# Routed experts in tiles of two widths, and expert offsets added to the ranks by a matmul

## The reference, cut to what matters

```python
gate = xf @ gate_w                                   # 4096 x 8
weights, sel = jax.lax.top_k(gate, k=2)
weights = jax.nn.softmax(weights, axis=-1)
h = einsum('ecd,td->tec', dense_1_w, xf) + dense_1_b  # 256 -> 2*512, each expert
h = swiglu(h)
y = einsum('edf,tef->ted', dense_2_w, h) + dense_2_b  # 512 -> 256
out = sum over the two selected experts of weight * y
x = x + gb * out
```

## Time and profile before

| | |
|---|---|
| median of 3 runs | 625.39 us (624.7 to 627.05) |
| profiled execution, its own time | 623.77 us |
| its span, first to last instruction | 622.0 us |
| TensorE busy | 566.1 us, 91% |
| VectorE busy | 492.8 us, 79% |
| POOL busy | 318.5 us, 51% |
| chain that ended last | 67% PE, 22% DVE |

### The profile page before, as it was taken

How to read it: one execution, slowest core, us unless ns; L and a number is a source line. 1 busy time by engine, 2 the same in 40 slices (tenths; PEclk the granted TensorE clock), 3 DMA queues, 4 the chain that set the end, 5 groups by cost and what they waited for, 6 DMA issues and landing times.

```text
span 622.0 us, 13215 instructions
## 1 busy us (share of the span) xinstructions
PE 566.1 (91%) x4005; PEld 429.5 (69%) x4006; DVE 492.8 (79%) x1067; ACT 300.9 (48%) x497; POOL 318.5 (51%) x211
## 2 busy tenths in 40 slices
PE   5998999999999967459899999999999999999982
PEld 5444555655656534326788888888888888888871
DVE  1258879899999899897588888888888888888881
ACT  3677568789688762732433333333333333333320
POOL 0004031442414421002458888888888888888554
PEclk9799889899899886776899999999999999999996
DMA  9204273653645448533667777777777777777633
GB/s 316 95 18 170 68 202 102 202 144 115 199 102 170 119 129 308 175 29 95 157 101 138 137 137 137 138 134 132 128 137 134 135 133 134 135 131 130 95 35 35
DMA packets 86942, 82.93 MB, mean 133 GB/s; under 512 B 48628, under 2 KB 76276, under 8 KB 86648
## 3 DMA queue, kind: packets, MB, share of 16 engines
q0 software_dynamic: 18480, 34.51, 31.8%
q1 hardware_dynamic: 67128, 47.07, 26.8%
q10 hardware_dynamic: 1296, 0.87, 0.4%
HBM read 45.90 MB, written 23.15 MB: 111 GB/s over the span
## 4 chain that ended last, share of the span: by engine, by line
PE 67%; DVE 22%; issue 4%; ACT 3%; POOL 2%; DMA 1%; POOLq 0%; ACTq 0%; DVEq 0%
PE ps L738 32%; PE ps L757 16%; PE ps L496 7%; DVE region L1204 3%; PE ps L555 2%; POOL region L1617 1%; PE ps L651 1%; DVE region L1251 1%; DVE region L1168 1%; DVE region L1219 1%; PE ps L595 1%; PE ps L591 1%; DVE region L1388 1%; PE ps L434 1%; DVE region L1213 1%
## 5 line engine op out<-in xcount | busy, mean ns | idle before, releaser
L738 PE MATMUL ps<-region,w_sb 128*128 128x256 f16 x1872 | 212.4, 274 | 2.3 <-ACT region L983 2.3
L738 PEld LDWEIGHTS ps<-region,w_sb 128*128 x1872 | 183.6, 98 | 24.7 <-issue 2.5
L1647 POOL DMA_INDIRECT out_rows<-w_stage,region x78 | 149.6, 1918 | 44.5 <-DVE w_stage L1564 22.6
L1637 POOL DMA_INDIRECT region<-h_scratch,region x78 | 106.1, 1361 | 75.6 <-DVE region L1506 48.5
L1532 DVE TENSOR_SCALAR region<-ps,region 128x256 f32<-128x256 f32 x156 | 68.1, 479 | 57.4 <-PE ps L738 57.4
L757 PE MATMUL ps<-region 128*128 x936 | 110.2, 275 | 3.6 <-DVE region L1546 3.6
L757 PEld LDWEIGHTS ps<-region 128*128 128x128 f16 x936 | 92.1, 99 | 15.5 <-issue 4.2
L1088 ACT ACTIVATE region<-region 128x1024 f16<-128x1024 f32 x39 | 41.3, 1058 | 126.9 <-DVE region L1540 126.9
L1076 ACT ACTIVATE region<-ps,region 128x256 f32<-128x256 f32 x156 | 65.2, 470 | 72.4 <-PE ps L738 72.3
L496 PE MATMUL ps<-region 128*128 128x512 f32 x192 | 86.4, 607 | 4.0 <-ACT region L851 4.0
L1617 POOL TENSOR_TENSOR region<-region 128x512 f32<-128x512 f32 x30 | 37.3, 1267 | 91.9 <-DVE region L1231 91.9
(11 more groups left out here) (209 smaller groups left out, 686.5 us busy)
## 6 DMA issues: line engine op xcount, KB each, us to landing
w_stage<-in_w SPq DMA_DIRECT2D x20, 512.0 KB, 3.9
region<-in_x SPq DMA_DIRECT2D x8, 512.0 KB, 8.0
out_rows<-region SPq DMA_DIRECT2D x8, 512.0 KB, 3.1
h_scratch<-gb_bc SPq DMA_DIRECT2D x4, 1024.0 KB, 7.2
h_scratch<-region SPq DMA_DIRECT2D x8, 512.0 KB, 3.2
region<-region POOLq DMA_DIRECT2D x7, 512.0 KB, 5.6
region<-in_ramp SPq DMA_DIRECT2D x1, 2064.0 KB, 11.1
region<-in_w SPq DMA_DIRECT2D x4, 512.0 KB, 7.6
```

Source lines behind the costliest of these rows:

```text
L738: mm = pe.matmul(ps[:, GV + 2 * half + a, (f % 2) * MT:(f % 2 + 1) * MT], w, xg_t[:, s, xa * KD + k, :], start=(n == 0), stop=(n == 3 * KD ...
L1637: G.indirect_dma_start(out=xg_rows[:, t % XG, u, :], out_offset=None, in_=h_scratch, in_offset=bass.IndirectOffsetOnAxis(ap=gather_idx[:, ...
L1647: G.indirect_dma_start(out=out, out_offset=bass.IndirectOffsetOnAxis(ap=scatter_idx[:, at:at + 1], axis=0), in_=y_sb[:, t % 2, u, :], in_o ...
```

## The change

Tiles now come in two widths. The first 32 tiles (`BIG`) have 256 slots, the last seven (`SMALL`) 128: 71 columns of 128 slots in place of 78. An expert with `n` pairs gets `floor(ceil(n/128)/2)` big tiles, and a small one if `ceil(n/128)` is odd. In a small tile `up` has its 48 matmuls with 128 moving columns, `down` has 12 matmuls, and there is one gather, one transpose and one scatter. Nine tiles, not three, are written out behind the loop.

To rank: no rank is made early. TensorE first takes the eight totals (`rank_totals`), VectorE works out the offsets and puts them in `base_b`, and TensorE adds them within the same accumulation that makes the counts, for all 64 columns (`rank_all`). VectorE then lifts the pairs that belong in small tiles (`lift`), picks the own counts, and splits them once for all pairs. `low_hot` is made in the four parts of the loop, and each part of `place_pairs` waits for its own. The experts of the tiles are found while TensorE places the pairs, but packed into `te_word` only after the second part of `gather_idx`. ScalarE rounds block 6 (`split_rows`) before it copies the first half of the last block.

```diff
-MOE_TILES = PAIRS // MT + EXPERTS - 1
-SLOT_COLS = SUB * MOE_TILES
+BIG = PAIRS // MT
+SMALL = EXPERTS - 1
+MOE_TILES = BIG + SMALL
+SLOT_COLS = SUB * BIG + SMALL
+def subs(t):
+    return SUB if t < BIG else 1
...
-            def rank_early():
-                pe.wait_ge(early_ready, 1)
-                cols = rot(("row", LAST, 0))[:, 0:EXPERTS * C1].rearrange("p (e c) -> p e c", e=EXPERTS)
-                pe.matmul(cols, tri_b[:, 0, :], picked[:, :, 1:C1 + 1], start=True, stop=False)
-                pe.matmul(cols, tri_b[:, 1, :], ahead[:, :, 0:C1], start=False, stop=True).then_inc(early_mm, 1)
+            def rank_totals():
                 pe.wait_ge(late_ready, 1)
+                pe.wait_ge(row_ready, NBLK)
+                pe.matmul(rot(("row", LAST, 0))[:, 0:EXPERTS], tri_b[:, 1, :], ahead2[:, :, C2],
+                          start=True, stop=True).then_inc(late_mm, 1)
+            def rank_all():
+                pe.wait_ge(base_ready, 1)
+                bank = rot(("lo", NBLK, 3)).rearrange("p (e c) -> p e c", e=EXPERTS)
+                for at, n, hot, before in ((0, C1, picked, ahead), (C1, C2, picked2, ahead2)):
+                    cols = bank[:, :, at:at + n]
+                    pe.matmul(cols, tri_b[:, 0, :], hot[:, :, 1:n + 1], start=True, stop=False)
+                    pe.matmul(cols, tri_b[:, 1, :], before[:, :, 0:n], start=False, stop=False)
+                    mm = pe.matmul(cols, tri_b[0:1, 1, :], base_b[0:1, :].unsqueeze(2).to_broadcast([1, EXPERTS, n]),
+                                   start=False, stop=True)
+                mm.then_inc(rank_mm, 1)
...
+            dve.wait_ge(rank_mm, 1)
+            done(V.tensor_tensor(lift, counts, from_e.unsqueeze(2).to_broadcast(every), ALU.is_ge))
+            done(V.tensor_tensor(lift, lift, lift_e.unsqueeze(2).to_broadcast(every), ALU.mult))
+            done(V.tensor_tensor(lift, lift, counts, ALU.add))
+            own = sel.rearrange("p c e -> p e c")
+            done(V.tensor_tensor(own[:, :, 0:C1], lift[:, :, 0:C1], picked[:, :, 1:C1 + 1], ALU.mult),
+                 V.tensor_tensor(own[:, :, C1:], lift[:, :, C1:], picked2[:, :, 1:C2 + 1], ALU.mult))
+            done(V.tensor_reduce(rank, sel, AX_X, ALU.add))
...
-                        mm = pe.matmul(ps[:, GV + 2 * half + a, (f % 2) * MT:(f % 2 + 1) * MT], w,
-                                       xg_t[:, s, xa * KD + k, :],
+                        mm = pe.matmul(ps[:, GV + 2 * half + a, (f % 2) * MT:(f % 2) * MT + wide], w,
+                                       xg_t[:, s, xa * KD + k, 0:wide],
...
-                    pool.wait_ge(scattered[1 - t % 2], 16 * SUB * ((t + 1) // 2))
+                    pool.wait_ge(scattered[1 - t % 2], moved(t - 1, 2))
```

More of the change, by code:

```diff
@@ L61, with col_of, moved @@
 RE, IM = 0, 1
+def subs(t):
+    return SUB if t < BIG else 1
+def col_of(t):
+    return SUB * min(t, BIG) + max(t - BIG, 0)
+def moved(t, ring, first=0):
+    return 16 * sum(subs(i) for i in range(first + (t - first) % ring, t + 1, ring))
 def psum_plan():
@@ L744, in up, with down @@
                         between()
-            def down(t, s, e):
+            def down(t, s, e, parts=SUB):
                 pe.wait_ge(hid_ready, t + 1)
-                if not isinstance(t, int) or t >= 2:
+                if not isinstance(t, int):
                     pe.wait_ge(y_ready, SUB * (t - 1))
-                for u in range(SUB):
+                elif t >= 2:
+                    pe.wait_ge(y_ready, col_of(t - 1))
+                for u in range(parts):
                     n = 0
@@ L781, in _ @@
             six_turns(0, first=True)
-            with pe.Fori(1, SIX) as n:
+            with pe.Fori(1, ROUNDS) as n:
                 six_turns(n)
[L784 to L790, removed]
+            for t in range(XG * ROUNDS, MOE_TILES):
+                if t % XG == 0:
+                    e = experts(t // XG)
+                if t + 1 < MOE_TILES:
+                    up(t + 1, (t + 1) % 2, e[t % XG + 1], moved(t + 1, 2, 2), wide=P * subs(t + 1))
+                down(t, t % 2, e[t % XG], parts=subs(t))
         @block.scalar
@@ L1444, in _ @@
             V.tensor_tensor(pw_row[:, :, 1], pw_tmp[:, 1, :], pw_row[:, :, 0], ALU.subtract).then_inc(pw_ready, 1)
-            dve.wait_ge(late_mm, 1)
-            bank = rot(("lo", NBLK, 3))
-            cols = bank[:, 0:EXPERTS * C2].rearrange("p (e c) -> p e c", e=EXPERTS)
-            count, tiles, in_use, upto, begin = (small[:, i, :] for i in range(5))
-            done(own_counts(C1, PCOLS, cols, picked2),
-                 V.tensor_scalar(count.bitcast(I32), bank[:, EXPERTS * C2:EXPERTS * (C2 + 1)], float(MT - 1), None,
-                                 ALU.add))
@@ L1459, in _ @@
-            for first, last, hot in ((0, C1, picked), (C1, PCOLS, picked2)):
-                n = last - first
-                done(V.tensor_tensor(sel[:, first:last, :].rearrange("p c e -> p e c"), hot[:, :, 1:n + 1],
-                                     begin.unsqueeze(2).to_broadcast([P, EXPERTS, n]), ALU.mult))
-            done(V.tensor_reduce(offset, sel, AX_X, ALU.add))
-            done(V.tensor_tensor(hi16, rank_hi, offset, ALU.add))
-            low_hot(C1, PCOLS)
+            dve.wait_ge(rank_mm, 1)
@@ L1484, in _ @@
-            done(V.tensor_copy(words, sixes[:, 0:SIX + 1, 0]))
-            for m in range(1, XG):
-                done(V.scalar_tensor_tensor(out=words, in0=sixes[:, 0:SIX + 1, m], scalar=float(8 ** m), in1=words,
-                                            op0=ALU.mult, op1=ALU.add))
-            V.scalar_tensor_tensor(out=te_word, in0=sixes[:, 1:SIX + 2, 0], scalar=float(8 ** XG), in1=words,
-                                   op0=ALU.mult, op1=ALU.add).then_inc(tiles_ready, 1)
+            ends, sixes = upto.unsqueeze(1), tile_e.rearrange("p (n m) -> p n m", m=XG)
@@ L1490, in _ @@
+            done(V.tensor_tensor(tile_e[:, BIG:MOE_TILES], tile_e[:, BIG:MOE_TILES], odd_e, ALU.add))
             done(*[V.tensor_scalar(spare[:, u:u + 1], pcol, float(TOKENS + u * P + 1), None, ALU.add)
```

221 lines of the change are left out of this document (114 added, 107 removed).

## The result

Three runs of the changed kernel took 600.69 us (600.44 to 601.39), 0.960 of the time before, with an interval of 0.957 to 0.9635: 24.7 us faster. Six later runs gave 600.83; sixteen runs of the kernel before, taken with them, gave 623.79, so that pair lies 23.0 us apart (0.9645). The forecast was 600, its range 594 to 606.

A forecast was written before the change was run, and what follows sets the result against it. TensorE was taken to bound the expert stage; 22.9 us there plus 2.3 from routing and ScalarE's order gave 25.2 off, 600.2 us from the 625.39 median, said as 600. Its own range was 597 to 604, for 8 in 10 594 to 606.

The forecast's parts named there:

- The sequencer paces the small tiles: Small tiles on TensorE: address instructions at 0.124 us each set the pace, 5.45 us per tile against 7.86 for a big one.
- E: Time at which up(31) ends in the expert stage, from which the prediction counts; 546.42 us before the change.
- The stall of `down(31)`: Expert stage after up(32): down(31) waits 0.6 us for the hidden rows of tile 31.
- A scatter chain takes 4.3. Both lie under 5.45.: Small tiles: VectorE's some 3.8 us and a scatter chain's 4.3 are covered by the sequencer's pace of 5.45 us.
- the tail: After up(38) at E + 39.3: last down, scaling and scatters, with the data end at E + 49.4.
- the sum: Whole kernel: 22.9 us from the expert stage plus 2.3 from routing and ScalarE's order, 25.2 us off.
- Rival A: Small tiles: the array paces at 4.0 us, then the scatter chain binds; gain 26.1 + 2.3, 597 us, chance 0.15.
- Rival B, the clock: Small tiles: gaps between matmuls drop TensorE's clock to 1.2 GHz, 8.0 us a tile; 614 us, chance 0.07.
- ScalarE's order, 1.2 us: Before routing: rounding block 6 ahead of the first-half copy shortens VectorE's 1.83 us wait; 1.2 us gained, bounds 0 and 1.8.
- Routing, 1.1 us: Routing stage: placing starts at 276.5 not 279.0 and ends at 286.7 not 287.8, with VectorE the pacer; 1.1 us gained.
- Rivals C, D and E: C: routing gives nothing, 602 to 604, 0.12; D: small tiles not cheaper, 623, 0.03; E: late transposes, slower, 0.03.

The follow-up runs named there:

- e1: Changed kernel with expert 0's weights at fixed addresses in the seven small tiles, so no register instructions there; 602.4 us, 0.964 of before.
- e2: Changed kernel with each weight address written over a byte view, one register addition per address in all 39 tiles; 601.21 us, 0.963 of before.
- e3: Changed kernel with sixteen more address instructions in each small tile's up, 48 in place of 32; 616.76 us, 0.989 of before.
- e11: Kernel before the change with only ScalarE's order changed, split_rows(6) ahead of last_residual(0); 623.19 us, 1.000 of before.
- e12: The changed kernel itself run and profiled once more; 600.83 us, 0.9645 of before.
- e9: Changed kernel with fixed weight addresses in small tiles and their rows stored by plain transfers without waiting for each other; 590.47 us, 0.947 of before.
- e7: Changed kernel with four small tiles processed among the big ones and weight addresses of one register addition; 601.72 us, 0.963 of before.
- e5: Changed kernel with one-addition weight addresses, small tiles' rows stored by plain transfers without waiting for the one before; 596.21 us, 0.956 of before.

## Why the prediction was right, point by point

- **The sequencer paces the small tiles.** Right, by e1, e2 and e3. Period 5.63 against 5.45 taken: an instruction costs 0.13 us rather than 0.124, `down` 1.48 rather than 1.3. `up(38)` ended at 584.73 = E + 40.9, not 39.3.
- **The stall of `down(31)`.** Right: it began at E + 5.98 (predicted 5.9).
- **"A scatter chain takes 4.3. Both lie under 5.45."** This is the term that was mis-sized, and with it the tail. The scatter-adds of the small tiles followed each other in 4.6 to 5.7 us even in the changed kernel, and those of tiles 32, 34 and 35 waited for the landing of the one before. In the tail the sum had 4.3 from the scatter of tile 37 to the last; it was 4.69 (587.93 to 592.62). And tile 37 was itself late: issued 3.2 us after `up(38)` ended, where the sum has 2.4. Part of that is `hidden(38)`, which VectorE has ahead of tile 37's rows and which ended 0.3 us after `down(37)`. Data end at E + 52.1 instead of E + 49.4: the expert stage gave 20.2 by this count, not 22.9. Of the 2.7 missing, 1.6 are there by `up(38)`, 1.1 come in the tail.
- **Rival A** had the right mechanism for what lies below the sequencer, and the wrong price: it had tile 31's scatters landed at E + 16 and seven more at 4.3 us, and a gain 3.2 us above the forecast's. With the sequencer out of the way (e1) they landed at E + 19.8 (565.62, with E at 545.85), the next seven started 4.5 to 5.5 us apart, and the stage took 304.7, no less than with the sequencer. The two limits are about equal here.
- **Rival B, the clock.** Did not happen: 1.00 over the small tiles at 22.66 of 23.48 us busy. In e1 it was 1.00 until 578 too, while pairs ran 0.056 us apart. It fell where TensorE had waited: in the last 6.3 us (0.80), and in e1 from 578 on (0.73), behind a wait of 2.55 us.
- **ScalarE's order, 1.2 us.** The wait went from 1.83 to 0.16 as reckoned, but 1.83 was the price at a low clock. Counted from the end of VectorE's `unbind` (243.70 before), the first `up` came after 53.7 us before and 53.0 in e11: 0.7, so the term was half a microsecond too high.
- **Routing, 1.1 us.** Too low. By the same count the two profiles of the changed kernel have 50.6 and 50.05, so 2.4 to 2.9 are the routing's, and it made good what the order did not give. The steps were close, each priced a little too high: `lift` 0.69 each (0.72 taken), the parts 2.58 us apart (2.65), the last burst over at 285.18 (286.7). VectorE is the pacer there, as said.
- **Rivals C, D and E.** None happened. Routing gave 2.4 to 2.9 us, a small tile took 5.63 us and not 7.9, and between `up(33)` and `up(38)` the chain has TensorE idle for 0.61, 0.10 and twice 0.05 us only, none of it behind a transpose.
- **The sum.** 25.2 us were predicted. The stage gave 20.7 and what stands ahead of it, counted from `unbind`, 3.1 in that profile; 20.5 and 3.7 in e12's. That is 23.8 to 24.2, and the medians differ by 24.7, or by 23.0 in the later runs. That 600.69 came within 0.5 us of the 600.2 of the sum is in part luck. The expert stage gave over 2 us less and the part ahead 1 us more, and the 625.39 from which the sum was taken off lay 1.6 us above the median of the sixteen later runs of the kernel before.

## What to carry to other kernels

- When work per instruction shrinks, price the instructions that make its addresses. They were free under 256 columns (0.109 us) and set the pace under 128: 0.13 us per register instruction, 32 for 48 matmuls.
- A second limit just below the first must be priced as carefully as the first. Here two chains of about equal length ended the kernel; taking away the register instructions alone gained nothing, taking away both 7.8 us, 9.6 with the cheaper last transfer. A chain that waits for each landing is read from its start-to-start times, not from POOL's busy time.
- Compare stages from a common row: whole runs of one kernel differed by 5.6 us, the expert stage by 0.7.

## What the runs showed of the hardware

- A register instruction on TensorE's sequencer took 0.118 us with one addition (e2) and 0.130 to 0.134 with fused operations (changed, e3), though its own record is 32 or 46 ns.
- Weight load and 128-column matmul pairs with fixed addresses ran at 0.056 us over 48 of them, at the full clock (e9).
- A scatter-add of 128 rows of 1 KB, each behind the landing of the last, repeated every 4.4 to 4.5 us at best (e1, e7): 3.6 to 3.8 from issue to landing (POOL's 1.55 in it) and 0.7 to the next issue.
- From the last issue to the end of the span it took 6.0 to 6.1 us with a scatter-add (changed, e1, e2) and 4.3 with a plain store of the same rows (e5, e9).
